# Differential-attention kernel: the transposed differences of a head copied out of two PSUM banks by one ScalarE instruction, ahead of the second exponential

## What is computed

```python
scores = einsum('bhqd,bhkd->bhqk', q, k) + causal      # 32 score heads, Dh = 16
probs  = softmax(scores).reshape(bsz, 16, 2, S, S)
diff   = probs[:, :, 0] - lambda_full * probs[:, :, 1]
attn   = einsum('bhqk,bhkd->bhqd', diff, v)            # then an RMS norm per head, and Wo
h      = gelu(x2 @ sign_quantised(w1).T + b1)
out    = h @ sign_quantised(w2).T + b2
```

## Time and profile before

| | |
|---|---|
| median of 3 runs | 4307.65 us (4298.69 to 4309.7) |
| the profiled execution | 4298.3 us, its span 4296.5 us |
| busy share of the span | PE 81%, DVE 79%, ACT 67%, POOL 33% |
| one batch, from the spacing of a line that runs once in a tile | 518.8 us |
| the tiles t = 0 to 7 of the third batch | 55.3, 47.6, 58.3, 59.6, 66.3, 72.6, 75.9, 83.2 us |

### The profile page before, as it was taken

How to read it: one execution, slowest core, us unless ns; L and a number is a source line. 1 busy time by engine, 2 the same in 40 slices (tenths; PEclk the granted TensorE clock), 3 DMA queues, 4 the chain that set the end, 5 groups by cost and what they waited for, 6 DMA issues and landing times.

```text
span 4296.5 us, 81536 instructions
## 1 busy us (share of the span) xinstructions
PE 3484.7 (81%) x23454; PEld 2095.0 (49%) x23454; DVE 3382.8 (79%) x6194; ACT 2880.2 (67%) x6784; POOL 1437.2 (33%) x1564
## 2 busy tenths in 40 slices
PE   2688888888888887888788888888878878888886
PEld 1355544455445454545544544445544555444553
DVE  6788977888678886888767887778877889778881
ACT  1577766777567775677756777667766777567772
POOL 1243233332332324433343323432234432333323
PEclk6899999999999999999999999999999999999998
DMA  3100011000011001100011000101011000111000
GB/s 130 41 18 30 19 33 33 31 17 29 25 33 33 18 30 33 33 20 28 21 33 33 26 27 18 39 25 33 20 34 33 25 23 20 34 33 33 15 29 12
DMA packets 146817, 128.38 MB, mean 30 GB/s; under 512 B 66608, under 2 KB 117680, under 8 KB 145840
## 3 DMA queue, kind: packets, MB, share of 16 engines
q1 hardware_dynamic: 146352, 122.79, 8.8%
HBM read 67.61 MB, written 55.12 MB: 29 GB/s over the span
## 4 chain that ended last, share of the span: by engine, by line
PE 41%; DVE 20%; issue 20%; ACT 12%; POOL 5%; DMA 1%; SPq 1%; DVEq 1%; ACTq 1%; POOLq 0%
PE M L837 9%; DVE NM L682 6%; PE M L887 6%; PE SP_ L852 6%; PE F L924 6%; PE F L909 5%; PE DP L864 4%; DVE NM L690 3%; ACT E L554 3%; ACT DT L566 2%; ACT L571 2%; PE M L831 2%; DVE CC L702 1%; PE DX L864 1%; PE SP_ L853 1%
## 5 line engine op out<-in xcount | busy, mean ns | idle before, releaser
L554 ACT ACTIVATE E<-SP_,NM 128x256 f32<-128x256 f32 (+7 forms) x2048 | 1520.4, 743 | 1020.3 <-DVE NM L690 533.8
L852 PE MATMUL SP_<-KST,QST 96*128 96x512 f16 (+3 forms) x3072 | 838.2, 344 | 459.2 <-ACT E L554 385.4
L682 DVE TENSOR_REDUCE NM<-SP_ 128x1 f32<-128x896 f32 (+3 forms) x1024 | 1031.9, 1017 | 225.0 <-PE SP_ L853 218.5
L705 DVE SCALAR_TENSOR_TENSOR E<-E,CC 128x512 f32<-128x512 f32 (+7 forms) x1024 | 942.2, 920 | 36.2
L864 PE MATMUL DP<-ident,E 128*128 128x128 f32 x3328 | 585.1, 292 | 112.8 <-DVE E L705 97.2
L852 PEld LDWEIGHTS SP_<-KST,QST 96*128 96x128 f16 x3072 | 277.9, 101 | 793.8 <-ACT E L554 531.1
L690 DVE TENSOR_REDUCE NM<-SP_ 128x2 f32<-128x1024 f32 (+3 forms) x512 | 419.4, 819 | 244.8 <-PE SP_ L853 239.5
L566 ACT ACTIVATE DT<-DP 128x512 f32<-128x512 f32 (+3 forms) x1024 | 524.8, 513 | 127.8 <-PE DP L864 121.4
L837 PE MATMUL M<-WQKV,WT 128*128 128x512 f32 x1040 | 538.4, 611 | 10.3 <-DVE TOK L746 5.3
L909 PE MATMUL F<-X2H,W1Q 128*128 128x256 f16 x2048 | 501.4, 283 | 39.4 <-ACT HP L613 21.7
L864 PEld LDWEIGHTS DP<-ident,E 128*128 128x128 f32 x3328 | 389.8, 149 | 277.8 <-issue 125.8
(11 more groups left out here) (94 smaller groups left out, 4726.9 us busy)
## 6 DMA issues: line engine op xcount, KB each, us to landing
scratch<-SPL SPq DMA_DIRECT2D x65, 576.0 KB, 2.8
QST<-scratch SPq DMA_DIRECT2D x390, 64.0 KB, 2.4
X<-in_x SPq DMA_DIRECT2D x66, 256.0 KB, 2.7
out<-SQ SPq DMA_DIRECT2D x64, 256.0 KB, 2.0
KST<-scratch SPq DMA_DIRECT2D x390, 32.0 KB, 1.9
DT<-in_w2T SPq DMA_DIRECT2D x1, 4096.0 KB, 25.7
KST<-in_w1T SPq DMA_DIRECT2D x2, 1024.0 KB, 12.0
WQKV<-in_wqT SPq DMA_DIRECT2D x1, 1024.0 KB, 7.1
```

The costliest lines, as they stand in the source:

```text
L554: act.activation(dst, score_out(i, 2 * n + k, w), ACT.Exp, bias=NM[:, (2 * u + k) % 8:(2 * u + k) % 8 + 1], scale=1.0, accum_out=SUM[:, i ...
L682: nc.vector.tensor_reduce(NM[:, m:m + 1], score_out(i, 2 * n + k, P * (i + 1)), AX.X, ALU.max, negate=True).then_inc(max_ready, 1)
L705: nc.vector.scalar_tensor_tensor(out=E1[:, u % 4, 0:w], in0=E2[:, u % 2, 0:w], scalar=CC[:, u % 4:u % 4 + 1], in1=E1[:, u % 4, 0:w], op0=A ...
L852: pe.matmul(SP_[:, k[a // 512], 0:n], q, KST[0:ROWS, a // P:(a + n) // P, kk, :], start=True, stop=not last)
```

## The change

`DP` becomes one PSUM tensor of two banks (`DX` is gone; its address is now `DP[:, 1]`). `dt_copy` has no group any more: one ACTIVATE copies all t + 1 turned tiles of a head, up to 1024 columns, out of both banks, and adds 2 to `dt_ready` where there are two groups. It waits for the transposes of the last group. It is issued once per head, in the second half-step, ahead of the second exponential; before, the part from `DP` was issued in the first half-step, and the part from `DX` in the second, behind the exponential. Whatever ACT does in the even half-steps (WT at 6, T1 at 4 and 20, GELU at 0 or 14, HP at 6) stood behind the copy of `DP` and now stands ahead of the copy.

```diff
-        DP = ctx.enter_context(nc.psum_tensor("DP", [P, 512], F32))
-        DX = ctx.enter_context(nc.psum_tensor("DX", [P, 512], F32))
+        DP = ctx.enter_context(nc.psum_tensor("DP", [P, 2, 512], F32))
...
-            def dt_copy(b, i, n, g):
-                k0, k1 = 4 * g, min(4 * g + 4, i + 1)
+            def dt_copy(b, i, n):
+                g = groups(i) - 1
                 after(act, t_ready, b * N_T + tg(i, n, g) + 1)
                 if n % HALF == 0:
                     if n or i:
                         pi, pu = (i, 0) if n else (i - 1, 1)
-                        after(act, pv_done, b * N_PV + pg(pi, pu, min(g, groups(pi) - 1)) + 1)
+                        after(act, pv_done, b * N_PV + pg(pi, pu, groups(pi) - 1) + 1)
                     else:
                         after(act, pv_done, b * N_PV - 1)
-                act.activation(DT[:, k0:k1, n % HALF, :], (DP, DX)[g][:, 0:P * (k1 - k0)].rearrange("p (k q) -> p k q", q=P),
-                               ACT.Copy).then_inc(dt_ready, 1)
+                act.activation(DT[:, 0:i + 1, n % HALF, :],
+                               DP[:, :, :].rearrange("p g n -> p (g n)")[:, 0:P * (i + 1)].rearrange("p (k q) -> p k q", q=P),
+                               ACT.Copy).then_inc(dt_ready, g + 1)
...
                     old = T.before(s - 2)
+                    if old and h == 1:
+                        dt_copy(*old)
                     if T.attend:
                         exp(T, s, h)
-                    if old and (h == 0 or groups(old[1]) == 2):
-                        dt_copy(*old, h)
...
-                    ins = pe.transpose((DP, DX)[g][:, P * (k % 4):P * (k % 4 + 1)], E1[:, u % 4, P * k:P * (k + 1)], ident[:, :])
+                    ins = pe.transpose(DP[:, g, P * (k % 4):P * (k % 4 + 1)], E1[:, u % 4, P * k:P * (k + 1)], ident[:, :])
```

## The result

| | before | with the change |
|---|---|---|
| median | 4306.42 us (4298.69 to 4309.7, 4 runs) | 4355.47 us (4351.24 to 4360.57, 4 runs) |
| ratio | | 1.0116, 95% interval 1.0104 to 1.0128 |
| the profiled execution, its span | 4298.3 us, 4296.5 us | 4360.57 us, 4358.8 us |
| one batch | 518.8 us | 525.6 us |

The kernel became 49 us slower. Forecast were 19 us, and the range ended at 4346 us. The two profiled executions are 62 us apart, because the one before is the fastest of its kernel and the one with the change the slowest; their batches differ by 6.8 us. By the median length of each tile that is +1.8 us at t = 4, -0.3 at t = 5, +2.4 at t = 6, +3.8 at t = 7, -1.0 in t = 2 and 3 together, and +0.2 in t = 0. The forecast had +0.8 at t = 5 and next to nothing at t = 4.

What follows compares the result with a forecast made beforehand. No engine was taken as the bound, but the ACT-PE-DVE ring around each second exponential for t >= 4. Costs of 4.3 less gains of 1.9 us, 2.4 us per batch, 8 batches, 19 us on 4307.65: about 4326 us, range 4300 to 4346.

Steps and rivals of the forecast that it cites:

- (a): Half-steps 4 and 20, t = 4 to 7: the copy behind T1 delays the second exponential; cost 2.2 us per batch.
- (b): Half-step 6 of odd tiles (t = 5, 7): the exponential behind WT and the merged copy comes later; cost 1.4 us per batch.
- (d): Half-step 6: WT goes ahead of the copy, so it starts earlier and PE and DVE follow; gain 1.7 us per batch.
- (c): GELU at t = 5, 7 and half-step 0 of t = 6: the exponential comes later; cost 0.7 us per batch.
- (e): Start of t = 0: PE's second group of transposes is done about 1.1 us sooner; gain 0.2 us per batch.
- fourth rival: Every head of t >= 4 pays 0.11 to 0.43 us for the later exponential: 128 us, 4436 us; chance 0.03.
- No slack: The fourth rival: every head of t >= 4 pays for the later exponential, 128 us, 4436 us; chance 0.03.
- heavier: PE sets the pace of t = 0 to 4 and the earlier WT is lost: up to 38 us, 4346 us; chance 0.10.

Runs made afterwards that it cites:

- e9: The changed kernel with PE's long waits filled by matmuls whose result nobody reads: 4331.4 us, 0.0096 over the filled kernel before.
- e14: The changed kernel with PE's gaps filled, but heads 0 and 8 copied in two parts at their places and with their waits of before: 4309.79 us, 0.9990.
- e15: The filled changed kernel with heads 0, 8 and also 1 copied in two parts at their places and with their waits of before: 4306.33 us, 0.9988.
- e8: The kernel before with PE's gaps filled by matmuls never read and the half-step 15 product matmuls of odd tiles issued twice: 4293.64 us, 0.9966.
- e18: The same kernel as e8, the kernel before with PE's gaps filled, run again on another chip: 4296.38 us, 0.9968.
- e17: The changed kernel without any fill, but heads 0 and 8 copied in two parts at their places and with their waits of before: 4330.09 us, 1.0048.
- e7: The kernel before with five extra ACT copies of DP, once a batch, at half-step 6 of t = 7: 43 us longer for 19 us put in.
- e3: The changed kernel with the first FFN product's matmuls ahead of the GELU of t = 5 and 7 issued twice: 4351.61 us, 1.0122.
- e5: The kernel before with one extra ACT copy of DP, once a batch, at half-step 6 of t = 7: 17 us longer for 4 us put in.
- e10: The kernel before with PE's gaps filled and three extra ACT copies of DP a batch at t = 7, half-step 6: 0.0033 over e8, 14 us.

## Why the prediction was wrong

The direction and the places were right, the size of one term was not, and one effect was put at nothing. In the filled kernels:

```
                                        forecast          measured (95%)
(a) half-steps 4 and 20                 2.2 x 8 = 18      e9 - e14         31 us (23 to 39)
(b) - (d) half-step 6                   -0.3 x 8 = -2     e14 - e15         1 us (-5 to 7)
(c) - (e) and all other heads           0.5 x 8 = 4       e15 - e8, e18     9 us (2 to 16)
sum, with fill                          19                e9 - e8          41 us (32 to 50)
sum, without fill                       19                                 49 us (45 to 55)
```

**The term that failed is (a).** The slack of an exponential was taken as PE's lag plus DVE's lag. At half-step 20 the maxima indeed came as late as that gives, 0.49 us at t = 6 (forecast 0.47) and 0.24 at t = 7 (forecast 0.22), but PE's scores and the transposes behind them came 0.81 and 0.91 us late. Through the merged copy the transposes reach the next exponential without passing DVE, and in the end DVE too is 0.86 and 0.63 us late. At half-step 4 of t = 6 1.26 us were lost, 0.79 were forecast. These three places lost 2.75 us where the prediction had 1.48; in that proportion its 18 us would be 33, near the 31 that e14 gives back and the 29 of e17. The prediction had noted, as its fourth rival, that the exponential now waits for the copy and the copy for all transposes; it priced that for every head or for none, and not at the places where PE itself was late.

Two smaller things add to half-step 4 of t = 6. PE's product of the first group waits for a whole merged copy, 0.29 us. And T1 was followed by the copy 0.17 us later than before by the exponential; at half-step 20 it was not (0.29 us in place of 0.28). The first of them is not undone by e14 and e17, where head 15 is still copied in one: in e17 the second exponential of half-steps 4 and 5 of t = 6 starts 2.90 us behind the first (median of six batches), in the kernel before 2.51, in the changed one 3.77.

**What held.** The merged copy: 1022 ns against 1019. Part (b): the exponential at t = 7, half-step 7, is 2.11 us behind WT's start (1560.59 to 1562.70) where the prediction has 1.19 + 0.90 = 2.09. Part (c): 0.4 us more at the GELU of t = 7 (2.92 to 3.34 us of wait). Part (d) where it stands: t = 3 is shorter by 0.56 us against 0.48 forecast, t = 2 by 0.45 against 0.38. Part (e), at the start of t = 0, is the one gain that came out at nothing. PE with the change (as the earlier trace rows):

```profile
1637.04 1.97 PE L864 MATMUL DP<-ident,E 128*128 128x128 f32 x8 [4.78 <-ACT DT L565]
...
1640.35 3.64 PE L887 MATMUL M<-DT,V 128*32 128x256 f32 x32 [0.92 <-ACT DT L565]
```

From the row sum ahead of the GELU (1609.47 before, 1632.65 now, 23.18 us apart) the transposes are done 0.97 us sooner, 1.1 were forecast; but the product behind them starts at 1640.35, before at 1617.16, 23.19 us apart. This is also the case that the prediction's rows didn't show, transposes that are early at a bank the longer copy holds: 4.78 us of wait for all eight, where before four were done early and four waited 3.67. The Trainium skill, "PSUM — Partial Sum Buffer", section "PSUM bank collisions raise a hardware error", asks for that guard of the whole bank (strictly by bank and quarter of the partitions, and this copy reads all four); the extra microsecond of wait cost nothing here, and in t = 4 to 7 of the third batch the transposes never waited for a copy (only 1.8 us, four times, for a difference). "No slack" is out: without heads 0, 1 and 8 the changed kernel loses 9 us, not 128.

**What was put at nothing.** The forecast took a microsecond on the path for a microsecond of time, and gave no reason. Without fill it isn't: 4, 11 and 19 us put in cost 17, 33 and 43 us. The 19 us of e7 are the forecast's own sum, at one place without slack, and its 43 us (36 to 51) are nearly the 49 that were measured. So this effect alone could have given the number, and so could the longer path of some 41 us that the filled kernels show. The time of the changed kernel can't tell the two errors apart. What speaks for (a) apart from this is that with fill a known 11 us cost 14, while the forecast's 19 cost 41, and the rows of t = 6 and 7. How much of the 49 us belongs to each stays open, the more as the changed kernel, e14, e17 and e9 too stand on favoured lengths, so that a difference between two of them can be one step of 3.4 us a batch, 27 us.

By tile, the median over the batches, in us:

```
t                        0      1      2      3      4      5      6      7
forecast              -0.3    0.0   -0.4   -0.5   -0.1   +0.8   +1.2   +1.7
changed - before      +0.2    0.0   -0.4   -0.6   +1.8   -0.3   +2.4   +3.8
e9 - e8               -0.2    0.0   -0.9   -0.6    0.0   +1.3   +0.9   +3.1
```

With the fill t = 3 to 6 come near the forecast, and t = 7 does not. Without it t = 4 to 6 do not either; there the time at 1.2 GHz also moved between the tiles. Of the rivals, "heavier" (4346 us) came nearest, for another reason than its own: t = 2 and 3 did get shorter.

**Open** stays why the favoured lengths of a batch are 3.4 us apart and by what a small delay turns into such a step; why e3, with 10 us less at 1.2 GHz, kept its batch of 525.6 us; and how the 9 us that are left split between (c) and the other heads. The wait of PE's first product for the merged copy wasn't tried alone.

## What to carry to other kernels

When an instruction is moved from inside a wait to behind it, its whole length counts; and when two copies become one, list every semaphore that the larger one waits for and every reader that used to need only its first half. Slack must be followed along every customer of a late engine, not only along the ring one has in mind. Before a small change is judged, put a known delay into the kernel: here 19 us put in cost 43. Filling PE's gaps brought the cost of a known delay nearer to its length, and gave the fastest kernel.

## What the runs showed of the hardware

- The same idle time of PE can be followed by either clock: 2.92 us ahead of the scores of t = 7, with the granted clock 1.00 behind it in the kernel before, 0.72 in e5, where the tile was merely 0.67 us later.
- The length of a repeating batch settles on values 3.4 us apart (518.8, 522.2, 525.6 us) in kernels whose TensorE is at 1.2 GHz for 58 to 75 us of it. Two of them also show in kernels with 27 to 37 us at 1.2 GHz (518.8 in e10, 522.2 in e9), with single batches that lie elsewhere (520.0 and 515.7 in e14).
- A delay can cost more than its length: 4, 11 and 19 us cost 17, 33 and 43 us at a mean clock of 0.92; at 0.957 to 0.962, 11 us cost 14 (7 to 21).
- The time at 1.2 GHz does not tell the length: 68 us of a batch both in the kernel before (518.8 us) and in the changed one (525.6 us), 58 us in e3 (525.6 us).
- Matmuls that nobody reads make the kernel faster: 0.9966 and 0.9932 of the time before.
- An ACT copy of 1024 columns over two PSUM banks takes 1022 ns against 594 for 512 columns in one: the second half costs 428 ns, what it costs in the exponential (1118 - 692 = 426).
